# A state-space stage on one core: GpSimd takes both products with C and one of two dBu products, VectorE the other and the first batch's convolution

## The reference

```python
x = jnp.einsum('ed,bld->bel', in_proj_w, hidden_states)
xc = depthwise_conv(pad(x, 3), conv_w)                      # 4 taps along l
u = silu(xc + conv_b)
x_dbl = jnp.einsum('ke,bel->bkl', x_proj_w, u)              # dt_lo (16), Bm (16), Cm (16)
delta = softplus(dt_proj_w @ dt_lo + dt_proj_b)
A = -exp(A_log)
def step(state, (d_t, B_t, C_t, u_t)):                      # over l
    state = state * exp(d_t[..., None] * A) + (d_t * u_t)[..., None] * B_t[:, None, :]
    y_t = einsum('ben,bn->be', state, C_t)
y = (ys + D * u) * silu(z)                                  # z = layernorm(x)
```

## Time and profile before

| | |
|---|---|
| median of 3 runs | 2085.54 us (2084.83 to 2087.59) |
| profiled execution | 2088.46 us, span 2086.6 us |
| busy over the span | PE 1601.1 us, VectorE 1412.8, ScalarE 873.7, GpSimd 625.0 |
| state-space stage | 0 to 600 us |

### The profile page before, as it was taken

The page is one execution under the profiler, slowest core; times in us unless marked ns, Lnnn a source line. Parts: engine busy times, 40 slices in busy tenths (PEclk is TensorE's granted clock), DMA queues, the critical chain, the costliest instruction groups (busy, mean ns, idle before and its releaser), DMA issues. The chain is left out here.

```text
span 2086.6 us, 20794 instructions
## 1 busy us (share of the span) xinstructions
PE 1601.1 (77%) x6523; PEld 650.2 (31%) x6523; DVE 1412.8 (68%) x2163; ACT 873.7 (42%) x1125; POOL 625.0 (30%) x402
## 2 busy tenths in 40 slices
PE   4778886976651486289988988998899539898995
PEld 2232332432220232142244225323532213333332
DVE  3598898989986353558747855783687479655552
ACT  1546444463330110144643654364456234544452
POOL 0364555646635326130022003000300014242332
PEclk9898898988995799598999999999999769999998
DMA  4343444544557552400000000000000350000002
GB/s 154 102 140 111 134 129 115 141 117 134 143 125 174 142 101 77 161 1 1 2 11 1 2 12 1 1 1 12 1 1 1 78 117 0 1 1 0 0 1 81
DMA packets 65665, 131.77 MB, mean 63 GB/s; under 512 B 11536, under 2 KB 11792, under 8 KB 64800
## 3 DMA queue, kind: packets, MB, share of 16 engines
q1 hardware_dynamic: 49552, 94.73, 15.9%
q0 software_dynamic: 7168, 25.19, 5.4%
q10 hardware_dynamic: 8848, 10.58, 1.8%
HBM read 134.13 MB, written 12.87 MB: 70 GB/s over the span
## 5 line engine op out<-in xcount | busy, mean ns | idle before, releaser
L313 POOL TENSOR_TENSOR ssm_dBu<-ssm_du,ssm_BC 128x1024 f32<-128x1024 f32 x128 | 301.0, 2353 | 283.4 <-DVE ssm_du L328 107.4
L378 DVE TENSOR_TENSOR_SCAN ssm_dA<-ssm_dA,ssm_dBu 128x512 f32<-128x512 f32 x256 | 312.1, 1220 | 12.7 <-ACT ssm_dA L286 10.2
L223 PE MATMUL ssm_psY<-ssm_hC,ident 128*128 128x512 f32 x512 | 265.2, 645 | 69.6 <-DVE ssm_hC L335 69.4
L286 ACT ACTIVATE ssm_dA<-ssm_delta,ssm_negA 128x512 f32<-128x512 f32 x256 | 175.6, 692 | 271.4 <-DVE ssm_hC L335 271.2
L1186 DVE TENSOR_REDUCE soft_next_mx<-soft_next_psS 128x1 f32<-128x512 f32 x384 | 248.1, 686 | 50.8 <-PE soft_next_psS L1074 48.4
L1232 ACT ACTIVATE soft_next_Pr<-soft_next_psT 128x1024 f32<-128x1024 f32 x192 | 189.1, 1020 | 114.1 <-PE soft_next_psT L1101 113.9
L1449 DVE SCALAR_TENSOR_TENSOR mlp_first<-mlp_psQ,mlp_s_gu,mlp_first 128x512 f32<-128x512 f32 x176 | 131.9, 749 | 128.0 <-ACT mlp_first L1485 118.2
L1507 POOL TENSOR_TENSOR mlp_both<-mlp_first,mlp_third 128x512 f32<-128x512 f32 x88 | 125.3, 1424 | 283.3 <-DVE mlp_first L1449 143.1
L987 POOL TENSOR_TENSOR att_QS<-att_rot,att_QS 128x1024 f16<-128x1024 f32 x16 | 34.1, 2129 | 508.9 <-ACT att_QS L976 508.9
L335 DVE TENSOR_TENSOR ssm_hC<-ssm_dA,ssm_BC 128x512 f32<-128x512 f32 x256 | 172.7, 675 | 20.2 <-PE ssm_psY L223 20.2
L1534 PE MATMUL mlp_psD<-mlp_Wd,mlp_hT 128*128 128x512 f32 x352 | 170.7, 630 | 10.3 <-DVE mlp_hT L1430 10.3
(11 more groups left out here) (278 smaller groups left out, 2258.2 us busy)
## 6 DMA issues: line engine op xcount, KB each, us to landing
ssm_BC<-bc_rows SPq DMA_DIRECT2D x128, 512.0 KB, 4.8
moe_W<-in_masksT POOLq DMA_DIRECT2D x32, 512.0 KB, 9.1
deq_words<-in_gate_upT SPq DMA_DIRECT2D x32, 176.0 KB, 14.0
moe_XP<-sorted_rows ACTq DMA_DIRECT2D x4, 1030.0 KB, 22.7
X<-in_x SPq DMA_DIRECT2D x4, 1024.0 KB, 14.8
moe_XP<-results SPq DMA_DIRECT2D x4, 1024.0 KB, 9.0
out_x<-X SPq DMA_DIRECT2D x1, 4096.0 KB, 12.5
mlp_Wd<-in_downT ACTq DMA_DIRECT2D x8, 352.0 KB, 19.1
```

What stands on the lines that cost most here:

```text
L223: nc.tensor.matmul(psY[:, w, :], ident[:], hC[:, q % RC, :], start=False, stop=(n == DS - 1)).then_inc(summed, 1)
L286: nc.scalar.activation(dA[:, q % RA, :], delta[:, b % 2, e, :], ACT.Exp, scale=negA[:, e, n:n + 1]).then_inc(dA_done, 1)
L313: nc.gpsimd.tensor_tensor(dBu[:, g % RB], du[:, b % 2, hh * W:(hh + 1) * W, :], BC[:, g % RING, 0, :].unsqueeze(1).broadcast_to([P, W, S]) ...
L378: nc.vector.tensor_tensor_scan(dA[:, q % RA, :], dA[:, q % RA, :], dBu[:, g % RB, w, :], 0.0, ALU.mult, ALU.add).then_inc(h_done, 1)
```

## The change

- The products with C move from VectorE (L335, one of 128x512 per tile) to GpSimd (one of 128x1024 per group), which waits for both scans and, with hC four groups deep, for PE's sum of group g - 4.
- dBu is split: GpSimd makes tile 0, VectorE tile 1, each 128x512. GpSimd runs LEAD = 2 groups ahead with it, VectorE one group, between its two scans. dBu has four buffers.
- The scan writes into dBu in SBUF and no longer into dA; ScalarE and the reuse of dA wait for the scan (h_done), and SP, PE and the reuse of BC and dBu for the product with C (hC_done, now one count a group).
- Batch 0 is convolved otherwise: PE makes only the in-projection (16 passes where 64 were), and VectorE applies the four taps from PSUM into acc (one tensor_scalar and three scalar_tensor_tensor per channel tile, two tiles interleaved).
- w_tap, needed from batch 1 on, is made by GpSimd. The broadcast taps are loaded on SP behind waits for ctx and in_proj, ahead of the loads of X; the loads have semaphores of their own.
- Batch 0's softplus, sum and du are made for tiles 0 and 1 ahead of the loop, for 2 and 3 at j = 5 (ScalarE), 8 and 9 (VectorE). The layernorm's sqrt goes to j = 3, its end on VectorE to j = 4, silu(z) of batch 0 to j = 8.
- For the next batches: states on PE at j = 19 (was 20), steps at 21 and 23 (22, 24), u at 20 (21), the states' copy and its DMA both at 23 (24, 25), abs and relu at 25 and 26 (26, 28), Exp and Ln at 27 (29), add_delta at 27 (28), weigh_u at 28 (29).

The diff, cut to its core:

```diff
-    RING, RB, RA, RC = 5, 3, 4, 6
+    RING, RB, RA, RC = 5, 4, 4, 4
+    LEAD = 2
...
+                sp.dma_start(w_dt[:], ins["dt_proj_wT"]).then_inc(small_in, 16)
+                sp.wait_ge(ctx_in[0], 16)
+                sp.wait_ge(w_loaded, 16)
+                sp.dma_start(taps, ins["conv_wT"].partition_broadcast(P)).then_inc(taps_in, 16)
...
-                        sp.wait_ge(hC_done, W * (g - RING + 1))
+                        sp.wait_ge(hC_done, g - RING + 1)
...
-                pe.wait_ge(tap_done, DC)
-                pe.wait_ge(padded, 1)
                 pe.wait_ge(ctx_in[0], 16)
-                for m in range(DT * DC * CK):
-                    convolve(0, m)
+                pe.wait_ge(w_loaded, 16)
+                for e in range(DT):
+                    if e >= 2:
+                        pe.wait_ge(conv_done, e - 1)
+                    for c in range(CK):
+                        mm = nc.tensor.matmul(psI[:, e % 2, :], w_in[:, c, e * P:(e + 1) * P], ctxP[:, 0, c, PAD:], start=(c == 0), stop=(c == CK - 1))
+                    mm.then_inc(inproj, 1)
+                pe.wait_ge(small_in, 16 * 2)
...
+                    pe.wait_ge(hC_done, g + 1)
                     for w in range(W):
-                        q = W * g + w
-                        pe.wait_ge(hC_done, q + 1)
-                        nc.tensor.matmul(psY[:, w, :], ident[:], hC[:, q % RC, :], start=False, stop=(n == DS - 1)).then_inc(summed, 1)
+                        nc.tensor.matmul(psY[:, w, :], ident[:], hC[:, w, g % RC, :], start=False, stop=(n == DS - 1)).then_inc(summed, 1)
...
-                            act.wait_ge(hC_done, q - RA + 1)
+                            act.wait_ge(h_done, q - RA + 1)
...
+                    if b == 0 and j == 3:
+                        act.wait_ge(mv_done, 1)
+                        nc.scalar.activation(rstd[:], mv[:, :, 1:2], ACT.Sqrt).then_inc(rooted, 1)
+                    if b == 0 and j == 5:
+                        soften(0, range(W, DT), 2)
+                    if b == 0 and j == 8:
+                        for t in range(NT):
+                            gate_z(0, t)
...
+                def weigh_states(g, b, hh, n):
+                    if n == 0:
+                        pool.wait_ge(du_done, steps(b, hh))
                     pool.wait_ge(bc_in[g % RING], 16 * (g // RING + 1))
                     if g >= RB:
-                        pool.wait_ge(h_done, W * (g - RB + 1))
-                    nc.gpsimd.tensor_tensor(dBu[:, g % RB], du[:, b % 2, hh * W:(hh + 1) * W, :],
-                                            BC[:, g % RING, 0, :].unsqueeze(1).broadcast_to([P, W, S]), ALU.mult).then_inc(dBu_done, 1)
+                        pool.wait_ge(hC_done, g - RB + 1)
+                    nc.gpsimd.tensor_tensor(dBu[:, g % RB, 0, :], du[:, b % 2, hh * W, :], BC[:, g % RING, 0, :], ALU.mult).then_inc(dBu_done, 1)
+
+                def project(g):
+                    pool.wait_ge(h_done, W * (g + 1))
+                    if g >= RC:
+                        pool.wait_ge(summed, W * (g - RC + 1))
+                    nc.gpsimd.tensor_tensor(hC[:, :, g % RC, :], dBu[:, g % RB], BC[:, g % RING, 1, :].unsqueeze(1).broadcast_to([P, W, S]),
+                                            ALU.mult).then_inc(hC_done, 1)
+
+                pool.wait_ge(taps_in, 16)
+                pool.wait_ge(w_loaded, 16)
+                for k in range(DC):
+                    nc.gpsimd.tensor_tensor(w_tap[:, k], w_in, taps[:, k].unsqueeze(1).broadcast_to([P, CK, D]), ALU.mult).then_inc(tap_done, 1)
+                order = list(passes())
+                for g, b, hh, n in order[:LEAD]:
+                    weigh_states(g, b, hh, n)
+                for g in range(TOTAL):
+                    if g + LEAD < TOTAL:
+                        weigh_states(*order[g + LEAD])
+                    project(g)
...
+                def convolve(e, k, last):
+                    if k == PAD:
+                        dve.wait_ge(inproj, e + 1)
+                        ins_ = nc.vector.tensor_scalar(acc[:, e, :], psI[:, e % 2, :], par[:, e, k:k + 1], None, ALU.mult)
+                    else:
+                        chain.wait(last)
+                        late = PAD - k
+                        ins_ = nc.vector.scalar_tensor_tensor(out=acc[:, e, late:], in0=psI[:, e % 2, 0:S - late], scalar=par[:, e, k:k + 1],
+                                                              in1=acc[:, e, late:], op0=ALU.mult, op1=ALU.add)
+                    if k == 0:
+                        ins_.then_inc(conv_done, 1)
+                        return None
+                    return chain.mark(ins_)
+
+                def weigh_states(g, b, hh, n):
+                    if n == 0:
+                        dve.wait_ge(du_done, steps(b, hh))
+                    dve.wait_ge(bc_in[g % RING], 16 * (g // RING + 1))
+                    if g >= RB:
+                        dve.wait_ge(hC_done, g - RB + 1)
+                    nc.vector.tensor_tensor(dBu[:, g % RB, 1, :], du[:, b % 2, hh * W + 1, :], BC[:, g % RING, 0, :], ALU.mult).then_inc(dBu1_done, 1)
...
-                        nc.vector.tensor_tensor_scan(dA[:, q % RA, :], dA[:, q % RA, :], dBu[:, g % RB, w, :], 0.0, ALU.mult, ALU.add).then_inc(h_done, 1)
-                        if q >= 1:
-                            project(q - 1)
+                        nc.vector.tensor_tensor_scan(dBu[:, g % RB, w, :], dA[:, q % RA, :], dBu[:, g % RB, w, :], 0.0, ALU.mult, ALU.add).then_inc(h_done, 1)
+                        if w == 0 and g + 1 < TOTAL:
+                            weigh_states(*order[g + 1])
...
+                        add_delta(0, range(W, DT), 2)
+                    if b == 0 and j == 9:
+                        weigh_u(0, range(W, DT), 2)
```

More of the change, by code:

```diff
@@ L113, in stage_ssm @@
         X4 = X[:].rearrange("p (b t) d -> p b t d", t=NT)
-        w_in = hC[:, 0:2]
-        taps = dBu[:, 0:2].rearrange("p a w s -> p (a w) s")
+        w_in = hC[:, 0, 0:CK]
+        taps = delta[:, 1]
         ctx_in = [sem(f"ctx_in{i}") for i in range(B)]
@@ L264, in _, with soften @@
-                act.wait_ge(w_loaded, 16 * 6)
+                def soften(nb, es, k):
+                    part = acc[:, es[0]:es[-1] + 1, :]
+                    act.wait_ge(abs_done, DT * nb + es[-1] + 1)
+                    nc.scalar.activation(part, part, ACT.Exp, scale=-1.0).then_inc(e_done, 1)
+                    act.wait_ge(e_done, k)
+                    nc.scalar.activation(part, part, ACT.Ln, bias=1.0).then_inc(l_done, 1)
+                act.dma_start(w_in, ins["in_proj_wT"].rearrange("(c p) e -> p c e", p=P)).then_inc(w_loaded, 16)
@@ L267, in _ @@
-                nc.scalar.activation(rstd[:], mv[:, :, 1:2], ACT.Sqrt).then_inc(rooted, 1)
+                act.wait_ge(par_in, 16)
                 for e in range(DT):
                     gate_u(0, e)
-                for t in range(NT):
-                    gate_z(0, t)
                 keep_states(0)
@@ L275, in _ @@
                     split_step(0, e)
-                soften(0)
+                soften(0, range(0, W), 1)
                 act.wait_ge(A_done, 2)
@@ L279, in _ @@
                     j = hh * DS + n
[L280 to L281 removed]
+                    if n == 0:
+                        act.wait_ge(delta_done, steps(b, hh))
                     for w in range(W):
@@ L292, in _ @@
                                 gate_z(b + 1, t)
-                        if j == 24:
+                        if j == 23:
                             keep_states(b + 1)
-                        if j == 25:
                             send_states(b + 1)
[L297 to L301, removed]
+                        if j == 25 or j == 26:
+                            e = 2 * (j - 25)
+                            split_step(b + 1, e)
+                            split_step(b + 1, e + 1)
+                        if j == 27:
+                            soften(b + 1, range(DT), b + 1 + HALVES)
             @block.gpsimd
@@ L330, in project, with add_delta @@
[L330 to L335 removed]
+                def add_delta(nb, es, k):
+                    dve.wait_ge(l_done, k)
+                    dve.wait_ge(relu_done, DT * nb + es[-1] + 1)
+                    part = delta[:, nb % 2, es[0]:es[-1] + 1, :]
+                    nc.vector.tensor_tensor(part, part, acc[:, es[0]:es[-1] + 1, :], ALU.add).then_inc(delta_done, 1)
@@ L352, in add_results @@
                         nc.vector.tensor_tensor(xe, xe, psY[:, w, :].rearrange("p (t e) -> p t e", e=P), ALU.add).then_inc(added, 1)
-                dve.wait_ge(w_loaded, 16 * 6)
-                for k in range(DC):
-                    nc.vector.tensor_tensor(w_tap[:, k], w_in, taps[:, k].unsqueeze(1).broadcast_to([P, CK, D]), ALU.mult).then_inc(tap_done, 1)
+                dve.wait_ge(par_in, 16)
+                for pair in range(0, DT, 2):
+                    last = [None, None]
+                    for k in reversed(range(DC)):
```

(11 more changed lines are left out.)

85 lines of the change are left out of this document (40 added, 45 removed).

## The result

The kernel after takes 2102.65 us (2101.1 to 2104.96), the kernel before 2085.84 us on the same chip: a ratio of 1.0082, interval 1.0069 to 1.0094. It is 0.8% slower; 2071.5 was forecast, and 2102.65 lies outside the range. The profiled execution of after took 2101.5 us, its span is 2099.3.

The account below looks back on a forecast made before the run. VectorE bound the state-space stage from 82 us on; after the change GpSimd would: 51.6 + 128 x (3.53 + 0.50) + 0.5 + 11.4 + 1.8 = 581.1. Stage -14 us, so 2071.5 us, range 2060 to 2083.

Parts of the forecast that it names:

- The start: Before the state-space loop: GpSimd's first dBu at 51.6 us instead of 79.56, uncertain by 4 us either way.
- The bound moves to GpSimd, 3.53 us a group without contention: State-space loop: GpSimd's 512-column dBu and 1024-column product with C total 3.53 us, above VectorE's former 3.43.
- Contention 0.50 a group: State-space loop: VectorE's dBu product with both inputs in SBUF stops GpSimd for 0.50 us a group, between 0.33 and 0.68.
- rival 2: State-space loop: GpSimd is stopped for VectorE's whole product, 0.68 us a group, big ones at 2.3; 2097 us, chance 0.12.
- rival 3: State-space loop: VectorE's product costs GpSimd nothing, as the Mode Summary rule gives; 1994 us, chance 0.07.
- Each fits, and 1.2 us a group is won back: VectorE's extra loop work fits its spare 1.2 us a group; it may be 4 to 5 us late before GpSimd stands.
- ScalarE ... beside two groups of slack: nothing: ScalarE in the loop: batch 0's sqrt, soften and gate_z, up to 5.5 us with table loads, cost no time.
- Big sums 1.9 each: L323 and L328 on VectorE, two in each of three batches, stop busy GpSimd 1.9 us each, 11.4 in all.
- PE and hC's ring at zero: At each half, PE's sums free hC four groups deep in 16 us where 17.5 are allowed: narrowly no cost.
- rival 4: PE holds up hC's ring at each half, +20 us; 2091 us, chance 0.08.
- 56 passes less on PE: Batch 0's convolution at the start: PE's saved passes can't be hidden, so a start that doesn't shorten was excluded.
- The tail: Stage's end behind the last product with C: 4.2 us before, growing by 1.0 for the second pair of passes.

## Why the prediction was wrong, step by step

- **The start** (51.6 forecast): 48.82, inside its 4 us. The nine kernels with this start have their first dBu at 48.8 to 51.1, so the 2.8 us in the forecast's favour are partly chance.
- **The bound moves to GpSimd, 3.53 us a group without contention**: right, 3.54 in the three kernels without such a product of VectorE's.
- **Contention 0.50 a group**: 0.45 on GpSimd's instruction, plus 0.13 of waiting for the scan, 4.11 for 4.03. The contention was sized nearly right: its 0.05 less gives back 6.4 us, and the wait for the scan, for which nothing was forecast, costs 16.5; together they are the 9.9 us above. The pace even stayed under the 4.15 that was to be the sign of being wrong. That it stops GpSimd for the product's whole 0.68 (rival 2) is refuted: its 2097 lies nearest to the result by luck. No contention (rival 3) is refuted too.
- **"Each fits, and 1.2 us a group is won back"**: the step that failed. The cushion behind it was already wrong by its own numbers: 4.0 + 1.2 less 2.8 is 2.4 us and not 4 to 5. And I read the earlier trace rows as a price that only GpSimd pays. There VectorE's L1430 had begun 0.21 us ahead of GpSimd, so it showed only the case in which VectorE is first. In the loop of after GpSimd is hardly ever between instructions, VectorE mostly comes second, and waits: 1.93 instead of 0.68, so that the 1.2 us of spare time were gone (VectorE busy 100.00 of 100 us), and GpSimd waits 0.13 us a group for the scan.
- **"ScalarE ... beside two groups of slack: nothing"**: failed with it, though not only by it. It costed the work that was added for ScalarE, and not u's wait for PE, which the move from j = 21 to 20 sets four us earlier while PE's skip passes come no sooner. "Two groups of slack" would be 8 us: in after VectorE's wait of 5.6 us for dA cost GpSimd 4.4. The gaps cost 13.3 us; with the product behind both scans they still cost 11.3, with the old places under 1.
- **Big sums 1.9 each**: 1.95, right.
- **PE and hC's ring at zero** (rival 4 has them at +20): right. L342 waited for PE 0.5 us in all. PE's lateness behind a half came in by another way, through ScalarE's u.
- **"56 passes less on PE"**: 48, 16 for 64. It is in no sum.
- **The tail** was 0.9 us too short.

The prediction weighed two sentences of the Trainium skill. That of the GPSIMD Engine Reference, Specifications (shared interfaces, contention with VectorE instructions of two SBUF inputs) agrees with every kernel here: 1.94 us for L393, 0.66 with one input in PSUM. Advanced Engine Details and Errata, Mode Summary, says that GpSimd's instructions and VectorE's of two-port modes "will interfere/block eachother", and names no others. The direction, each other, agrees with 1.94 and 1.72 us above; the limit to these modes does not.

The stage is 10.1 us longer, the median 16.8. Behind the stage the profiled execution of after took 2.6 us more (1489.0 against 1486.4), 2.5 of it before the attention stage begins; the profiled execution of before lies 2.6 above its median and that of after 1.2 below; the rest is rounding and the time outside the span. Why the part behind the stage took longer stays open.

## To carry to other kernels

Before two engines share out elementwise work, list where each operand lies: an instruction of VectorE with two SBUF inputs beside a busy GpSimd costs both engines, one with an input in PSUM costs neither, and it is better to move another product than this one. A row that shows contention shows one order of arrival; ask what happens when the other engine is first, and don't count spare time on either until then. When a wait of one engine for another is moved earlier, check what the other is doing at the new place.

## What the hardware showed that was not expected

- VectorE's 128x512 product with two SBUF inputs is held until GpSimd's current instruction is over: 1.94 us for 0.67 (2.83 behind a fresh L343). With one input in PSUM it takes 655 to 666 ns in all 127.
- GpSimd pays 0.35 to 0.51 us for such a product, and 1.95 for a 128x2048 sum, in the instruction that it begins while VectorE's is running or just getting in. It pays nothing in one that it was in already, and nothing while VectorE's stays held.
- The hold can last longer than one instruction: sums of 128x1024 took 8.7 to 8.8 us over four boundaries in three kernels, two of 128x2048 took 8.3 over three. Others got in at the first. What decides at a boundary isn't settled.
